# Second attention: the score units for the maxima are placed ahead of every exponential unit and value block, and value blocks move between the exponential units

## The reference

```python
Q, K, V = split_heads(x @ Wq.T), split_heads(x @ Wk.T), split_heads(x @ Wv.T)   # 16 heads of 8
Q, K = rope(Q), rope(K)
logits = einsum('bhnd,bhmd->bhnm', Q, K) / sqrt(8)
logits = where(causal, logits, -inf)
probs = softmax(logits)
attn = einsum('bhnm,bhmd->bhnd', probs, V)
return merge_heads(attn) @ Wo.T
```

## Time and profile before

| | us |
|---|---|
| median of 3 runs | 2238.51 |
| lowest and highest run | 2227.88, 2258.29 |
| the profiled execution, its own time | 2239.11 |
| its span in the profile | 2237.4 |
| TensorE busy, share of the span | 2044.1, 91% |
| VectorE busy | 1766.5, 79% |
| ScalarE busy | 1372.6, 61% |
| mean granted TensorE clock | 0.965 |

### The profile page before, as it was taken

One profiled execution on the slowest core, in us unless ns is written; L12 is line 12 of the kernel. 1 busy time (PEld: TensorE's weight loads), 2 busy tenths in 40 slices (PEclk: granted clock), 3 DMA queues, 4 the chain that ended last, 5 costly groups with the idle time before them and its releaser, 6 DMA issues. The chain is left out here.

```text
span 2237.4 us, 45576 instructions
## 1 busy us (share of the span) xinstructions
PE 2044.1 (91%) x16998; PEld 1112.2 (50%) x16998; DVE 1766.5 (79%) x2383; ACT 1372.6 (61%) x3435; POOL 1235.6 (55%) x599
## 2 busy tenths in 40 slices
PE   5677899999999997899999999967899999999997
PEld 2224556555555553444444444424555555555553
DVE  6986889899899993567777777707899899899993
ACT  8455566666666664346566566655666766766663
POOL 0117778777777772524121221137777777787770
PEclk9799999999999999789999999989999999999999
DMA  2004112112111110502211211122111111111111
GB/s 62 0 2 126 35 34 46 37 35 48 35 39 44 35 34 26 163 3 86 73 42 47 50 39 39 28 70 73 30 44 39 36 44 42 34 44 39 35 34 43
DMA packets 85473, 101.38 MB, mean 45 GB/s; under 512 B 13504, under 2 KB 60552, under 8 KB 83208
## 3 DMA queue, kind: packets, MB, share of 16 engines
q1 hardware_dynamic: 82824, 96.77, 17.3%
q10 hardware_dynamic: 2432, 1.70, 0.3%
HBM read 33.94 MB, written 10.49 MB: 20 GB/s over the span
## 5 line engine op out<-in xcount | busy, mean ns | idle before, releaser
L848 POOL TENSOR_TENSOR ffn_RN<-ffn_SS,ffn_mhalf 128x16 f32<-128x16 f32 x128 | 372.5, 2910 | 272.8 <-DVE ffn_SS L794 272.4
L2003 DVE TENSOR_REDUCE attn_b_NX<-attn_b_s 128x1 f32<-128x512 f32 (+3 forms) x608 | 365.5, 656 | 144.6 <-PE attn_b_s L1696 143.7
L842 POOL TENSOR_TENSOR ffn_QK<-ffn_T 128x1024 f32<-128x1024 f32 x128 | 421.1, 3290 | 21.6 <-DVE ffn_T L742 21.5
L589 ACT ACTIVATE ffn_PB<-ffn_s,ffn_NM 128x128 f32<-128x128 f32 x1024 | 360.5, 390 | 100.7 <-DVE ffn_NM L764 100.7
L1921 ACT ACTIVATE attn_b_PT<-attn_b_s 128x1024 f32<-128x1024 f32 (+1 forms) x320 | 290.1, 938 | 193.3 <-PE attn_b_s L1730 193.1
L633 ACT ACTIVATE ffn_SQ<-ffn_w 128x1024 f32<-128x1024 f32 x128 | 131.1, 1024 | 314.6 <-DVE ffn_T L742 314.3
L378 PE MATMUL ffn_w<-ffn_Wqkv,ffn_H 128*128 128x512 f32 x512 | 248.0, 607 | 12.9 <-ACT ffn_SQ L633 5.6
L836 POOL TENSOR_TENSOR ffn_PB<-ffn_PB,ffn_RDEN 128x1024 f32<-128x1024 f32 x128 | 243.7, 1904 | 25.1 <-DVE ffn_RDEN L727 25.1
L589 ACT ACTIVATION_READ_ACCUMULATOR ffn_PB<-ffn_s,ffn_NM 128x1 f32 x1024 | 236.3, 231 | 0.0
L1696 PE MATMUL attn_b_s<-attn_b_KS,attn_b_QS 62*128 62x512 f32 (+3 forms) x768 | 225.1, 411 | 11.0 <-DVE attn_b_NX L2003 11.0
L758 DVE TENSOR_TENSOR ffn_QK<-ffn_QK,ffn_RN 128x1024 f32<-128x1024 f32 x128 | 218.6, 1708 | 0.4 <-POOL ffn_RN L848 0.3
(11 more groups left out here) (250 smaller groups left out, 3799.4 us busy)
## 6 DMA issues: line engine op xcount, KB each, us to landing
ffn_Voff<-ffn_Vcur SPq DMA_DIRECT2D x248, 128.0 KB, 2.3
ffn_H<-ffn_Y SPq DMA_DIRECT2D x64, 128.0 KB, 2.5
ffn_H<-ffn_U SPq DMA_DIRECT2D x64, 128.0 KB, 2.5
attn_b_QS<-attn_b_qk_parts SPq DMA_DIRECT2D x64, 128.0 KB
attn_b_KS<-attn_b_qk_parts SPq DMA_DIRECT2D x64, 128.0 KB
attn_b_qk_parts<-attn_b_RP SPq DMA_DIRECT2D x6, 1024.0 KB, 9.7
ffn_rope<-in_ffn_rope_dram SPq DMA_DIRECT2D x4, 1024.0 KB, 8.1
attn_b_rope<-attn_b_OS SPq DMA_DIRECT2D x252, 16.0 KB
```

Source lines behind the costliest of these rows:

```text
L589: last = act.activation(PB[:, x % 2, e, p, :], s_ps[:, e, p * P:(p + 1) * P], ACT.Exp, bias=NM[:, x % 2, e, p:p + 1], accum_out=DEN[:, x % ...
L842: pool.tensor_tensor(QK[:, x % 2, :, :, :].rearrange("p c q k -> p (c q k)"), T1[:, :, :, :].rearrange("p c h k -> p (c h k)"), T2[:, :, : ...
L848: pool.tensor_tensor(RN[:, x % 2, :], SS[:, x % 2, :], mhalf[:, :], ALU.pow).then_inc(rnorm, 1)
L2003: dve.tensor_reduce(at, bank, AX_X, ALU.max, negate=True).then_inc(s1_read, 1)
```

## The change

The list of score units, the exponential units and the value blocks stay what they are, and ACT's and DVE's programs are not touched. Only PE's order within a step changes. `OTHERS` lists the exponential units and value blocks of a step, with the value block of two pieces earlier behind the first exponential unit of a piece instead of ahead of it. Ahead of each item, score units are issued until their share of columns reaches the item's middle; the value blocks' columns are counted too.

```diff
-            def exp_columns(s, u):
-                return NPAR * width(s) * exp_units(s)[u][1]
-
+            def others(s):
+                at = [("exp", s, u, NPAR * exp_units(s)[u][1] * width(s)) for u in range(len(exp_units(s)))]
+                return at[:1] + [("values", s - PLAG, None, BG * width((s - PLAG) % NPIECE))] + at[1:]
+
+            OTHERS = [item for s in range(NPIECE) for item in others(s)]
             ALL_SCORES = sum(score_columns(slot, u) for slot in range(NT) for u in range(len(max_units(slot))))
-            ALL_EXPS = sum(exp_columns(s, u) for s in range(NPIECE) for u in range(len(exp_units(s))))
+            ALL_OTHERS = sum(cost for _, _, _, cost in OTHERS)
 
             def step(n, first):
                 scores = [(slot, u) for slot in range(NT) for u in range(len(max_units(slot)))]
-                done = columns = exps = 0
-                for s in range(NPIECE if 0 <= n < NG else 0):
-                    at = n * NPIECE + s - PLAG
-                    if at >= 0:
-                        value_block(*divmod(at, NPIECE))
-                    for u in range(len(exp_units(s))):
+                done = columns = passed = 0
+                for kind, s, u, cost in OTHERS if 0 <= n < NG else []:
+                    while done < len(scores) and columns * ALL_OTHERS < (passed + cost / 2) * ALL_SCORES:
+                        slot, v = scores[done]
+                        m = max_group(n, slot)
+                        if m is not None:
+                            begin_maxima(m, slot, v)
+                            max_unit(m, slot, v)
+                        if (slot, v) == (TURN_SLOT, 0) and n + 1 < NG:
+                            turn_unit(n + 1)
+                        columns += score_columns(slot, v)
+                        done += 1
+                    if kind == "exp":
                         exp_unit(n, s, u)
-                        exps += exp_columns(s, u)
-                        while done < len(scores) and columns * ALL_EXPS < exps * ALL_SCORES:
...
+                    elif n * NPIECE + s >= 0:
+                        value_block(*divmod(n * NPIECE + s, NPIECE))
+                    passed += cost
```

More of the change, by code:

```diff
@@ L1778, in step @@
             def step(n, first):
                 scores = [(slot, u) for slot in range(NT) for u in range(len(max_units(slot)))]
-                done = columns = exps = 0
-                for s in range(NPIECE if 0 <= n < NG else 0):
-                    at = n * NPIECE + s - PLAG
-                    if at >= 0:
-                        value_block(*divmod(at, NPIECE))
-                    for u in range(len(exp_units(s))):
-                        exp_unit(n, s, u)
-                        exps += exp_columns(s, u)
-                        while done < len(scores) and columns * ALL_EXPS < exps * ALL_SCORES:
[L1789 to L1797, removed]
+                done = columns = passed = 0
```

## The result

The changed kernel takes 2168.26 us (median of 4 runs, 2163.13 to 2174.03) against 2236.75 for the kernel before (4 runs). The ratio is 0.9681, with a 95% interval of 0.9605 to 0.9756: 68 us less, where 28 were predicted and 49 were the edge of the range. The profiled execution took 2163.13 us with a span of 2161.4, 76 less than the one before.

A forecast was written before the change was run, and what follows sets the result against it. No engine was taken as full: PE's order starved DVE and ACT, idling DVE 7.2 us a step. Thirteen steps at 1.9 us plus smaller gains in steps 0, 14 and 15 made 28, off 2239.1: 2211 us, range 2190 to 2238.

The forecast's parts named there:

- The bank rule: Score units around a value block: with three banks, two may lie up to 1.25 us apart without idling DVE.
- the rows' transfer: Rows made by the turn unit, needed by the next step's first exponential unit: cover shrinks from 2.0 to 1.2 us, holds.
- prices that the trace does not show: Single score unit ahead of an exponential unit, some 15 times a step: taken as 0.25 us, between 0 and 0.42.
- the 28.3: Forecast length in us of a full step at full clock, against 30.2 before, a gain of 1.9.
- Stretches 1, 2 and 4: Step start to value block 0, blocks 0 to 4, block 7 to end: forecast 4.87, 8.4 and 6.1 us.
- the walk: PE's new order through one step, timed with trace prices, the bank rule and ACT's times, in four stretches.
- stretch 3: Value block 4 to 7, 14 score units: forecast 8.9 us against 10.25, DVE needing 8.4.
- I count them unchanged: Half-clock stretches in the second attention, some 3 us each in steps 6 and 8, assumed to stay.
- The third rival: PE runs freer, DVE becomes the bound, half-clock stretches vanish: step 26.5 or less, 2183 us; chance 0.10.
- step 14's 1.3: Gain of 1.3 us counted for step 14, which has scores for its first half only.
- The first rival: Single score units cost PE what pairs saved, 0.42 us each: step 30.9, time 2249 us; chance 0.17.
- ACT's rival: ACT replaces DVE as bound, chained exponential units waiting: gain 0.9 us a step, time 2226 us; chance 0.15.

The follow-up runs named there:

- e4: Changed kernel with score unit and exponential unit exchanged wherever they follow a value block in that order; 2173.09 us, ratio 0.9719.
- e11: Changed kernel with two score banks used instead of three; 2247.63 us, ratio 1.0044.
- E6.0: Not a run: an exponential unit of piece 6 in a step; the prediction had it wait 0.4 us for an earlier unit's exponential.
- E0.0: Not a run: the first exponential unit of piece 0 in a step; its row, both matmuls, lasts 0.73 us in the changed kernel.
- e7: The kernel before, unchanged, run once more for its clock; 2233.12 us over 10 runs, ratio 1.0007.
- e2: Changed kernel with value blocks put back to the head of their pieces, so only the score units move; 2208.56 us, ratio 0.9887.
- e10: Only the score units moved, value blocks first in their pieces, with row maxima over 128 columns of each score matmul; 2192.85 us, ratio 0.9802.
- e5: Kernel before, its order kept, with row maxima over only the first 128 columns of each score matmul; 2180.47 us, ratio 0.9758.

## Why the prediction was wrong

- *The bound.* Right: no engine was full, and PE's order fed both others. The bank rule was right in size: 0.17 us of idle time at wide value blocks was said and 0.17 and 0.21 came; e4 and e11 bear it out.
- *The direction and the place.* Right: faster, most of it between V0 and V7 (1.4 and 1.1 us), V0's wait for the copy gone, the rows' transfer in time, PE waiting a little for ACT at E5.1 and E6.0.
- *The step that failed: "prices that the trace does not show", and with it the 28.3.* I charged 0.25 us for a single score unit ahead of an exponential unit, "since the next unit's first matmul cannot start before it either way". It can: E0.0's first matmul starts 0.01 us behind S0.0, on the other row half. An exponential unit with a single score unit on either side took 0.61 us, where one with a pair behind it took 0.58, so a single unit costs about half a pair, 0.13 instead of 0.25. I also kept 0.42 ahead of a value block, from rows with a stall in them, where it was 0.33 if PE had not waited. By an estimate from these rows that is 15 x 0.12 = 1.8 us a step, and up to 0.9 more at ten value blocks. The step was 27.0, 1.3 less than the sum. Stretches 1, 2 and 4 came out 0.4, 0.7 and 0.4 below the walk, and stretch 3, where DVE binds, 0.2 above it. I put the whole 1.3 to this term; the rows show the prices, but no run takes this term by itself, and in stretch 2 the walk's wait for ACT was an estimate too. 1.3 x 14.5 = 19 us of the 48 that the profiled pair gained beyond the forecast stand in it.
- *The second term that failed: the clock, "I count them unchanged".* They were not unchanged. Between 1005 and 1450 us the two profiles of the old order had clocks of 0.97 and 0.93, the changed kernel 1.00 up to 1400. That is 11 us in the profiled pair. In e7's profiled execution it is over 20: four of its fifteen intervals are 5.2 us above clean ones.
- *The third rival*, the free PE, named both causes, single units that hide beside the other row half and a clock without half-speed stretches, with a chance of 0.10. It had the step at 26.5 or less, 5 us for the clock and 2183; its own terms, 54 and 5 off 2239, give 2180.
- *The rest of the miss.* What follows the last turn unit (the end of step 14, and step 15) gave 6.5 us, where 0.5 and a part of step 14's 1.3 were counted. The 8.5 us before the first step are chance, in the profiled pair; the medians differ by 68 us, not 76.
- *What each part does.* The prediction counted the gain as DVE's idle time, and that fell. But the table above says that 1.1 of the 3.2 us a step are lost when DVE's load goes and 2.1 are left, so two thirds of the gain can be had on PE and ACT alone. Of these, 1.2 come with the value blocks' place. PE's waits for the copy are gone there; that ACT has a unit to work on while the value block runs is argued from its shorter waits, not shown apart. The 0.9 that the score units add to it without DVE's load have no cause shown.
- *The first rival* (2249, single units at 0.42) is refuted by the same rows, 0.61 us for an exponential unit and two single score units. The Trainium skill's rule on weight loads ("TensorE: Matmul & The Clock Gate", Part 3) stood beside it: by the rule a single score unit ahead of an exponential unit would cost PE the weight load that a pair hides. Here no such cost shows: e4's exchange puts a pair in place of the two single units behind V10, and V10 to V11 is 1.55 against 1.56.
- *ACT's rival* is there in small (0.28 and 0.18 us at E5.1 and E6.0), not as the bound.

**What stays open** is why the clock falls where it does. The kernel before (twice), e2 and e10 have 24 falls in their steps 1 to 14. Sixteen stand within half a microsecond of the end of a wait of 0.36 to 0.58 us for ACT's copy at V0 or V4, eight at the second or third of three single masked score units in a row ahead of V4. But neither place is enough for a fall. The kernel before waits 0.36 us or more at V0 in every step, also in step 7, which kept its full clock, and e5 has its 0.57 and 0.30 in every full step and no fall. All seven kernels profiled with the value blocks between the units and three banks, and the one with two, had no fall between steps 1 and 13; four profiles of five with the value block first had some, and e5 had none. Waits for banks alone don't do it (e11), nor are they needed (e10). That the change removed both places is shown; a rule for the clock is not.

## What to carry to other kernels

Price an instruction from rows in which its engine had not waited: here a score unit that followed a stall cost 0.42 us and the same one in a stream 0.33, and a sum made of such rows makes the new order look dearer than it is. Where units fill the array by halves, count matmuls on each half rather than units: a pair that is taken apart can find new partners in the unit between. A merged row that lasts longer than its neighbours (0.73 for 0.50) is the sign to look for. Where one in-order engine feeds two others, try the long block between two items for each consumer instead of ahead of them, and give the number of buffers a time (here, by the bank rule, three banks bridge 1.25 us, two 0.64). When a change closes gaps on TensorE, look for half-clock stretches that begin at those gaps, and give them a term of their own.

## What the runs showed of the hardware

Short waits can stand right ahead of a fall of the clock: 0.36 us of PE's waiting at V0 in the kernel before was followed by over 3 us at 1.2 GHz, though in step 7 a wait of 0.37 at the same place was not. The two-bank kernel, with PE recorded busy for 384.7 of 421 us, kept 2.4 GHz in all of them. The Trainium skill ("TensorE: Matmul & The Clock Gate", "Why this matters for your kernels") warns of idle gaps between bursts of matmuls; in these traces no wait of PE in the 5 us ahead of any of the 24 falls was longer than 0.58 us. An exponential unit on both row halves with a single score unit ahead of it and one behind took 0.61 us, hardly more than the 0.58 of the same three with the score units as a pair: the matmuls of one unit start 0.34 us apart (1171.14 and 1171.48), each beside a score unit on the other half.
